# TensorE's loop cut at another place of the tile, with its matmul steps at fixed slots of the instruction blocks

## Chip, cores and metric

One NeuronCore of a Trainium2 chip runs the whole kernel. The metric is the device time of one execution in microseconds; lower is better.

## What is computed

x is 8 sequences of 2048 rows of 512 float32 values. One layer of causal linear attention with 16 heads of 32, a layer norm, a feed-forward part, and a second layer norm. Cut to its core, the reference is:

```python
q = exp(x @ Wq.T + bq); k = exp(x @ Wk.T + bk); v = x @ Wv.T + bv     # per head of 32
kv = cumsum(k[:, :, :, None] * v[:, :, None, :], axis=1)
k1 = cumsum(k, axis=1)
out = einsum('zsD,zsDd->zsd', q, kv) / sum(q * k1)
x = layernorm(x + out @ Wo.T + bo)
h = x @ weight @ aux_weight1 @ aux_weight2
x = layernorm(x + tanh(h + bias))
```

## The kernel before

A tile is 128 rows of one sequence. There are 128 tiles: NI = 16 positions times B = 8 sequences, and the eight sequences take turns, so tile t is position t // 8 of sequence t % 8. The running sums of a sequence (state, k1) stay on chip.

Each of the five engines has its own program, and semaphores alone tie them together. SyncE issues all the DMAs. VectorE does the scan of K, the transposes, the reciprocal, the sums and the norm statistics. ScalarE copies out of PSUM, takes exp and tanh, and applies the norms. GpSimd masks the scores and makes the low halves of split operands. A float32 product of 512 x 512 weights is done as three passes over rounded operands: high times high, high times low and low times high (`three_pass`, lines 309 to 315, lines 312 to 314 of it are the three matmuls). Each of its four steps k has three matmuls of 512 columns, and each matmul is two instructions of the engine, a weight load and the multiplication, so a step is 6 instructions.

`slot(c, k)` of the TensorE program (line 349) works on tile k of chunk c in this order:

- the denominators of the tile before and its product with the state (`denominators`, lines 368 and 372);
- the scores of the tile (line 425);
- the product of the masked scores of the tile before with V (`attend`, line 381);
- the state update of the tile two back (line 436);
- Q and K: one block each of the projections of the tiles four ahead (lines 450 and 459);
- V of the tile (line 467), the output projection of the tile before (line 396), the feed-forward product of the tile two back (line 408).

The first four groups are many small matmuls, 32 weight loads and 32 multiplications to a product; I call them the small part. The last five are `three_pass` calls, 24 instructions each.

Each engine runs its slots through `run_slots`: tiles -8 to 7 are written out, then a loop over chunks 1 to 13 has eight slots as its body (tiles 8 to 111), then tiles 112 to 129 are written out. In the compiled program before, TensorE's body is 3632 instructions: 453 to a tile (440 weight loads and multiplications and 13 waits of their own, the other waits ride on a matmul) and eight for the loop (the hint and five register updates at its head, an addition and the branch at its end). Within a tile the small part takes instructions 0 to 325, Q 326 to 351, K 352 to 376, V 377 to 400, the output projection 401 to 426 and the feed-forward 427 to 452.

The loop on TensorE:

```python
with nc.Fori(1, NI - 2, engines=(engine.engine,), hint_back_edge=True) as it:
    c = Chunk(it, engine)
    for k in range(B):
        slot(c, k)
```

Of the kernel before, what the change touches and what calls it, by code (L numbers as in the profile page):

```python
# [26 lines left out]
def linear_attention_ffn_kernel(nc, x, wqT, wkT, wvT, woT, bq, bk, bv, bo, w, a1T, a2, bf, out):  # L27
# [5 lines left out]
    P = 128  # L33
# [23 lines left out]
    with ctx:  # L57
# [250 lines left out]
        def _(pe):  # L308
            def three_pass(out, statH, statL, movH, movL):

                for k in range(NK):
                    nc.tensor.matmul(out, statH(k), movH(k), start=(k == 0), stop=False)  # L312
                    nc.tensor.matmul(out, statH(k), movL(k), start=False, stop=False)  # L313
                    last = nc.tensor.matmul(out, statL(k), movH(k), start=False, stop=(k == NK - 1))  # L314
                return last
# [33 lines left out]
            def slot(c, k):  # L349
                b = k % QUAD  # L350
                s = (k // QUAD) % 2
                ns = 1 - s
                cols = slice(b * P, (b + 1) * P)
                att = c.exists(k)
                prev = c.exists(k - 1)
                ffn = c.exists(k - 2)
                proj = c.exists(k + 4)
                heads = [(g, j, slice(g * HD, (g + 1) * HD), slice(j * HD, (j + 1) * HD))
                         for g in range(NK) for j in range(HG)]

                def denominators(n):

                    ts, tcols = (n // QUAD) % 2, slice(n % QUAD * P, (n % QUAD + 1) * P)

                    wait_before(pe, (qk1_ready, c.count(n + 1)), (o_ready, c.count(n)),
                                (state_ready, c.state_count(n - 1)))
                    for g, j, quarter, h in heads:
                        last = nc.tensor.matmul(den_ps[quarter, j, :], ones[h, :], qk1[h, g, :], start=True, stop=True)  # L368
                    last.then_inc(den_done, 1)
                    if c.reads_state(n):  # L370
                        for g, j, quarter, h in heads:
                            nc.tensor.matmul(num_ps[quarter, j, :], state[h, n % B, g, :], QT[h, ts, g, tcols],  # L372
                                             start=True, stop=False, skip_group_check=True)

                def attend(n):
                    wait(pe, v_ready, c.count(n + 1))
                    wait(pe, masked, c.count(n + 1))
                    for j in range(HG):
                        for g in range(NK):
                            f0 = g * P + j * HD  # L380
                            last = nc.tensor.matmul(num_ps[g * HD:(g + 1) * HD, j, :], V[:, n % 2, f0:f0 + HD],  # L381
                                                    A[:, n % 2, j, g, :], start=not c.reads_state(n),
                                                    stop=True, skip_group_check=True)
                    last.then_inc(num_done, 1)

                def output_projection():
                    if not ffn:
                        pe.wait_ge(woh_ready, 1)
                        pe.wait_ge(wol_ready, 1)
                    wait(pe, oh_ready, c.count(k))  # L390
                    wait(pe, ol_ready, c.count(k))

                    if att:
                        wait(pe, scores_out[3], c.count(k + 1))
                    wait(pe, r_ready, c.count(k - 1))
                    three_pass(oproj_ps, lambda f: oH[:, f, :], lambda f: oL[:, f, :],
                               lambda f: WoH[:, f, :], lambda f: WoL[:, f, :]).then_inc(oproj_done, 1)

                def feed_forward():
                    wait(pe, x1h_ready, c.count(k - 1))  # L400
                    wait(pe, x1l_ready, c.count(k - 1))

                    if proj:
                        wait(pe, q_ready, c.count(k + 5))
                    elif att:
                        wait(pe, scores_out[0], c.count(k + 1))
                    wait(pe, z_ready, c.count(k - 2))
                    three_pass(ffn_ps, lambda f: x1H[:, f, :], lambda f: x1L[:, f, :],
                               lambda f: WfH[:, f, :], lambda f: WfL[:, f, :]).then_inc(ffn_done, 1)

                if att and prev:
                    denominators(k - 1)
# [14 lines left out]
                if att and prev:  # L428
                    attend(k - 1)
# [10 lines left out]
                if proj:  # L440
# [15 lines left out]
                    if att:  # L456
# [4 lines left out]
                               lambda f: xTL[:, ns, f, :]).then_inc(kproj_done, 1)  # L461
                if att:
# [4 lines left out]
                    three_pass(v_ps, lambda f: xTH[:, s, f, cols], lambda f: xTL[:, s, f, cols],  # L467
                               lambda f: WvH[:, f, :], lambda f: WvL[:, f, :]).then_inc(v_done, 1)
                if att and not c.exists(k + 1):
                    denominators(k)  # L470
                    attend(k)
# [364 lines left out]
```

## Time and profile before

| | |
|---|---|
| median of 3 runs | 2349.64 us (2347.27 to 2354.92) |
| the profiled execution, its own time | 2354.96 us |
| its span in the trace | 2353.2 us |
| mean granted TensorE clock | 0.991 |
| PE busy | 2250.8 us, 96% |
| PE weight loads busy | 1833.2 us, 78% |
| DVE, POOL, ACT busy | 69%, 55%, 43% |

The profiled execution is the longest of those shown, 5.3 us over the median of the runs. A matmul's end in the trace is modelled, so the intervals between the starts of instructions are the safer measure, and the busy share of PE says only that it is seldom without work. Instructions themselves come from device memory by a DMA queue of their own, the page's queue of kind "instruction": its 235 packets of together 3.85 MB are 16 KB each, 256 instructions of 64 bytes. I call 256 instructions that begin at a multiple of 256 a block.

### The profile page before, as it was taken

To read this page: it belongs to the slowest core of one execution; us is meant where nothing else is said; L and a number is where in the kernel's file an instruction comes from. 1 tells how busy PE (TensorE), PEld (TensorE's weight loads), DVE (VectorE), ACT (ScalarE), POOL (GpSimd) and SP (SyncE) were. 2 spreads that over 40 slices of the span, in tenths; PEclk is the share of its full clock that TensorE was granted. 3 is DMA by queue.
4 is the path that set the end of the run, shared out by engine and by line. 5 is a ranking of instruction groups with operands and counts; after the bars stand their busy time and mean duration, and the time that the engine had idled before them with its cause. 6 is when DMAs were issued, how large, how long until landed. Compare 5 with 4: busy or idle time off the path is not lost.

```text
span 2353.2 us, 71216 instructions
## 1 busy us (share of the span) xinstructions
PE 2250.8 (96%) x27784; PEld 1833.2 (78%) x27784; DVE 1620.6 (69%) x2444; ACT 1012.5 (43%) x1683; POOL 1289.1 (55%) x1797
## 2 busy tenths in 40 slices
PE   3999999999999999999999999999999999999985
PEld 2778887878888888887878788787888878788864
DVE  3477776776776767767767767677777677677674
ACT  2344444444444444444444444444444444444442
POOL 1255555556555555555555555555555655555553
PEclk9999999999999999999999999999999999999997
DMA  5133333333333333333333333333333333333221
GB/s 156 46 101 107 108 108 107 104 108 109 105 110 103 109 109 104 109 108 100 113 105 105 105 107 109 104 105 107 110 104 109 109 100 107 111 101 113 69 68 55
DMA packets 294453, 242.74 MB, mean 103 GB/s; under 512 B 33329, under 2 KB 225841, under 8 KB 294193
## 3 DMA queue, kind: packets, MB, share of 16 engines
q1 hardware_dynamic: 294192, 238.69, 32.5%
q8 instruction: 235, 3.85, 0.7%
q14 instruction: 26, 0.20, 0.0%
HBM read 139.99 MB, written 98.57 MB: 101 GB/s over the span
## 4 chain that ended last, share of the span: by engine, by line
PE 94%; issue 2%; DVE 2%; ACT 1%; DMA 1%; POOL 1%; SPq 0%; POOLq 0%; DVEq 0%; ACTq 0%
PE SC L312 26%; PE SC L313 25%; PE SC L314 24%; PE SC L425 6%; PE ND L381 5%; PE ND L372 3%; PE ND L368 2%; PE ND L436 2%; DVE o L670 0%; PE ND L312 0%; PE ND L313 0%; PE ND L314 0%; DMA KT<-wkT 0%; DMA QT<-wqT 0%; ACT A L552 0%
## 5 line engine op out<-in xcount | busy, mean ns | idle before, releaser
L756 POOL TENSOR_SCALAR_AFFINE_SELECT A<-A 128x512 f32<-128x512 f32 x512 | 327.8, 674 | 313.2 <-ACT A L552 313.1
L670 DVE RECIPROCAL o<-ND 128x512 f32<-128x512 f32 x128 | 427.8, 3342 | 1.1 <-PE ND L381 0.9
L727 DVE TENSOR_TENSOR xres<-SC,xres 128x512 f32<-128x512 f32 x128 | 88.6, 692 | 457.0 <-PE SC L314 456.8
L750 POOL TENSOR_TENSOR oL<-o,oH 128x512 fp32r<-128x512 f32 x128 | 166.1, 1298 | 324.8 <-ACT oH L531 324.8
L542 ACT ACTIVATE WK<-xres,shift,rstd 128x512 f32<-128x512 f32 x128 | 104.4, 816 | 530.4 <-POOL shift L796 530.4
L552 ACT ACTIVATE A<-SC 128x512 f32<-128x512 f32 x512 | 264.7, 603 | 48.7 <-PE SC L425 48.6
L312 PE MATMUL SC<-xTH,WqH 128*128 128x512 f32 x512 | 211.3, 413 | 31.4 <-POOL xTL L785 27.3
L785 POOL TENSOR_TENSOR xTL<-xin,xTH 128x512 fp32r<-128x512 f32 x128 | 165.7, 1295 | 100.8 <-ACT xTH L580 100.7
L312 PE MATMUL SC<-WfH,x1H 128*128 128x512 f32 x512 | 201.4, 393 | 14.4 <-issue 7.8
L683 DVE TENSOR_TENSOR_SCAN WK<-ones,k,KT 128x128 f32<-128x128 f32 x512 | 207.7, 468 | 9.9 <-PE ND L368 9.9
L313 PE MATMUL SC<-xTL,WqH 128*128 128x512 f32 x512 | 201.2, 393 | 13.0 <-issue 13.0
L557 ACT ACTIVATE QT<-SC,bcol 128x512 f32<-128x512 f32 x128 | 88.4, 691 | 289.8 <-PE SC L314 289.8
L312 PE MATMUL SC<-WoH,oH 128*128 128x512 f32 x512 | 201.0, 393 | 9.8 <-issue 7.8
L312 PE MATMUL SC<-xTH,WkH 128*128 128x512 f32 x512 | 200.3, 391 | 7.7 <-DVE WkL L616 7.7
L312 PE MATMUL SC<-WvH,xTH 128*128 128x512 f32 x512 | 199.6, 390 | 2.7 <-ACT A L552 2.7
L314 PE MATMUL SC<-xTH,WqL 128*128 128x512 f32 x512 | 201.4, 393 | 0.0
L313 PE MATMUL SC<-WfL,x1H 128*128 128x512 f32 x512 | 200.8, 392 | 0.0
L314 PE MATMUL SC<-WfH,x1L 128*128 128x512 f32 x512 | 200.5, 392 | 0.0
L314 PE MATMUL SC<-WoH,oL 128*128 128x512 f32 x512 | 200.4, 391 | 0.0
L313 PE MATMUL SC<-WoL,oH 128*128 128x512 f32 x512 | 200.2, 391 | 0.0
L313 PE MATMUL SC<-xTL,WkH 128*128 128x512 f32 x512 | 200.0, 391 | 0.0
L314 PE MATMUL SC<-xTH,WkL 128*128 128x512 f32 x512 | 199.9, 390 | 0.0
(100 smaller groups left out, 5025.0 us busy)
## 6 DMA issues: line engine op xcount, KB each, us to landing
xin<-x SPq DMA_DIRECT2D x512, 64.0 KB, 1.8
xres<-x SPq DMA_DIRECT2D x128, 256.0 KB, 2.6
x_rows<-WK SPq DMA_DIRECT2D x128, 256.0 KB, 2.9
WK<-x_rows SPq DMA_DIRECT2D x512, 64.0 KB, 2.0
out<-WK SPq DMA_DIRECT2D x128, 256.0 KB, 2.1
k_rows<-WK SPq DMA_DIRECT2D x120, 256.0 KB, 2.0
WK<-k_rows SPq DMA_DIRECT2D x480, 64.0 KB, 1.9
QT<-wqT SPq DMA_DIRECT2D x4, 256.0 KB, 4.5
```

The source lines that it names most:

```text
L312: nc.tensor.matmul(out, statH(k), movH(k), start=(k == 0), stop=False)
L313: nc.tensor.matmul(out, statH(k), movL(k), start=False, stop=False)
L314: last = nc.tensor.matmul(out, statL(k), movH(k), start=False, stop=(k == NK - 1))
L381: last = nc.tensor.matmul(num_ps[g * HD:(g + 1) * HD, j, :], V[:, n % 2, f0:f0 + HD], A[:, n % 2, j, g, :], start=not c.reads_state(n), st ...
L425: last = nc.tensor.matmul(SC[:, j, g * P:(g + 1) * P], KT[h, s, g, cols], QT[h, s, g, cols], start=True, stop=True)
L542: nc.scalar.activation(x1[:, n % 2, :], xres[:, n % 2, :], ACT.Identity, bias=shift[:, 0:1], scale=rstd[:, 0:1]).then_inc(x1_ready, 1)
L552: nc.scalar.activation(A[:, k % 2, j, :, :].rearrange("p g q -> p (g q)"), SC[:, j, :], ACT.Copy).then_inc(scores_out[j], 1)
L670: nc.vector.reciprocal(o[:, :, :], den_ps).then_inc(recip_ready, 1)
L683: last = nc.vector.tensor_tensor_scan(qk1[:, g, :], ones[:, 0:1].to_broadcast([P, P]), KT[:, s, g, cols], k1[:, k % B, g:g + 1], ALU.mult, ...
L750: nc.gpsimd.tensor_tensor(oL[:, :, :], o[:, :, :], oH[:, :, :].bitcast(F32), ALU.subtract).then_inc(ol_ready, 1)
L756: last = nc.gpsimd.affine_select(out=A[:, k % 2, j, :, :], in_=A[:, k % 2, j, :, :], compare_op=ALU.is_ge, fill=0.0, base=0, pattern=[[0, ...
L785: nc.gpsimd.tensor_tensor(halves[1], xin[:, m % XIN, :].rearrange("p (t g q) -> p g t q", t=HG, q=HD), halves[0].bitcast(F32), ALU.subtrac ...
```

## The change

The TensorE `slot` is cut into three functions: `small` (denominators to state update), `queries_and_keys`, and `values_output_ffn`. The order of the instructions that compute is the same over the whole program. The loop on TensorE begins one tile's small part, Q and K later: these of tile 8 are written out ahead of it, the body is V, output projection and feed-forward of tile k and then small part, Q and K of tile k + 1, and after the loop the first written tile begins at V. The other engines keep `run_slots` as it was.

Inside the loop, and only there (`c.static()` is false), padding is asked for: V begins at slot 0 of a block of 256, the output projection at 40, the feed-forward at 80, and the steps k = 1, 2, 3 of each begin 10, 20 and 30 slots after its start. `addr_align` fills the slots up to the place with no-operations. `head_slot` puts the first instruction of the loop at slot 232 of a block, the loader branching over that gap once.

```diff
-            def three_pass(out, statH, statL, movH, movL):
+            def three_pass(out, statH, statL, movH, movL, place=None):
                 for k in range(NK):
+                    if place is not None and k > 0:
+                        pe.addr_align(256, offset=place + 10 * k, max_nops=255)
                     nc.tensor.matmul(out, statH(k), movH(k), start=(k == 0), stop=False)
...
+            def values_output_ffn(c, k):
...
+                v_place, o_place, f_place = (None, None, None) if c.static() else (0, 40, 80)
+
+                def align(place):
+                    if place is not None:
+                        pe.addr_align(256, offset=place, max_nops=255)
+
+                def output_projection():
+                    align(o_place)
...
+                def feed_forward():
+                    align(f_place)
...
                 if att:
+                    align(v_place)
...
-            run_slots(pe, slot, 8, 2, {-3: multiply_aux, -2: multiply_weight, -1: multiply_bv})
+            setup = {-3: multiply_aux, -2: multiply_weight, -1: multiply_bv}
+            for t in range(-8, B):
+                c, k = Chunk(t // B), t % B
+                small(c, k)
+                queries_and_keys(c, k)
+                values_output_ffn(c, k)
+                if t in setup:
+                    setup[t]()
+
+            small(Chunk(1), 0)
+            queries_and_keys(Chunk(1), 0)
+            with nc.Fori(1, NI - 2, engines=(pe.engine,), hint_back_edge=True, head_slot={pe.engine: 232}) as it:
+                c = Chunk(it, pe)
+                for k in range(B):
+                    values_output_ffn(c, k)
+                    small(c, k + 1)
+                    queries_and_keys(c, k + 1)
+            for t in range(NT - 2 * B, NT + 2):
+                c, k = Chunk(t // B), t % B
+                if t > NT - 2 * B:
+                    small(c, k)
+                    queries_and_keys(c, k)
+                values_output_ffn(c, k)
```

## Rows read from the trace of the kernel before

**Rows 1.** Page, part 4: the chain that ended last, shares of the span

```profile
PE 94%; issue 2%; DVE 2%; ACT 1%; DMA 1%; POOL 1%; SPq 0%; POOLq 0%; DVEq 0%; ACTq 0%
```

**Rows 2.** Groups of instructions: busy us, mean ns | idle before us <-releasers

```profile
L313 PE MATMUL SC<-xTL,WqH 128*128 128x512 f32 x512 | 201.2, 393 | 13.0 <-issue 13.0
...
L313 PEld LDWEIGHTS SC<-WoL,oH 128*128 128x128 f32 x512 | 96.9, 189 | 20.0
```

**Rows 3.** Timeline, PE, 1059 to 1066: start, us, instructions, [idle before <-releaser]

```profile
1059.83 0.52 PE L372 MATMUL ND<-QT,state 32*32 32x128 f32 x4
1060.77 0.50 PE L372 MATMUL ND<-QT,state 32*32 32x128 f32 x28 [0.43 <-issue]
1061.22 1.17 PE L425 MATMUL SC<-QT,KT 32*128 32x128 f32 x32
...
1063.65 0.47 PE L312 MATMUL SC<-xTH,WqH 128*128 128x512 f32 x1
1065.36 0.39 PE L313 MATMUL SC<-xTL,WqH 128*128 128x512 f32 x1 [1.23 <-issue]
```

**Rows 4.** Timeline, PE, a tile without idle time

```profile
1079.18 0.75 PE L372 MATMUL ND<-QT,state 32*32 32x128 f32 x32
1079.87 1.17 PE L425 MATMUL SC<-QT,KT 32*128 32x128 f32 x32
...
1082.31 0.47 PE L312 MATMUL SC<-xTH,WqH 128*128 128x512 f32 x1
1082.61 0.39 PE L313 MATMUL SC<-xTL,WqH 128*128 128x512 f32 x1
...
1087.85 0.39 PE L312 MATMUL SC<-WvH,xTH 128*128 128x512 f32 x1
...
1090.12 0.39 PE L313 MATMUL SC<-WvL,xTH 128*128 128x512 f32 x1
1090.34 0.39 PE L314 MATMUL SC<-WvH,xTL 128*128 128x512 f32 x1
1090.57 0.39 PE L312 MATMUL SC<-WoH,oH 128*128 128x512 f32 x1
```

**Rows 5.** Timeline, PE: first scores in the loop, two later tiles, first scores after it

```profile
223.40 1.17 PE L425 MATMUL SC<-QT,KT 32*128 32x128 f32 x32
...
1114.33 1.17 PE L425 MATMUL SC<-QT,KT 32*128 32x128 f32 x32
...
1201.33 1.17 PE L425 MATMUL SC<-QT,KT 32*128 32x128 f32 x32
...
2044.28 1.17 PE L425 MATMUL SC<-QT,KT 32*128 32x128 f32 x32 [1.10 <-issue]
```

**Rows 6.** Timeline, PE, 990.5 to 994.5: the stall in the fifth tile of the body

```profile
992.86 0.37 PE L436 MATMUL ND<-V,WK 128*32 128x32 f32 x24
993.65 0.27 PE L436 MATMUL ND<-V,WK 128*32 128x32 f32 x8 [0.42 <-issue]
```

**Rows 7.** Queues: packets, MB, share of 16 engines; windows 0:2353.2 (page) and 1061.22:1201.33

```profile
q8 instruction: 235, 3.85, 0.7%
...
q8 instruction: 15, 0.25, 0.8%
```

**Rows 8.** Queues, windows of 0.1 us from 990.9, 1057.3, 1062.9, 1066.8, 1080.9, 1084.9

```profile
q8 instruction: 1, 0.02, 81.7%
...
q8 instruction: 1, 0.02, 122.4%
...
q8 instruction: 1, 0.02, 60.0%
...
q8 instruction: 1, 0.02, 77.2%
...
q8 instruction: 1, 0.02, 92.8%
...
q8 instruction: 1, 0.02, 76.8%
```

**Rows 9.** Queues, windows of 0.1 us from 1185.0 and 1198.3

```profile
q8 instruction: 1, 0.02, 89.9%
...
q8 instruction: 1, 0.02, 64.6%
```

**Rows 10.** Timeline, PE, 1200 to 1206

```profile
1200.88 0.50 PE L372 MATMUL ND<-QT,state 32*32 32x128 f32 x28 [0.30 <-issue]
...
1205.46 0.40 PE L313 MATMUL SC<-xTL,WqH 128*128 128x512 f32 x1 [1.23 <-issue]
```

More of the change, by code:

```diff
@@ L347, in multiply_bv, with denominators @@
                 pe.wait_ge(consts_ready, 1)
-            def slot(c, k):
-                b = k % QUAD
+            heads = [(g, j, slice(g * HD, (g + 1) * HD), slice(j * HD, (j + 1) * HD))
+                     for g in range(NK) for j in range(HG)]
+            def denominators(c, n):
+                ts, tcols = (n // QUAD) % 2, slice(n % QUAD * P, (n % QUAD + 1) * P)
+                wait_before(pe, (qk1_ready, c.count(n + 1)), (o_ready, c.count(n)),
+                            (state_ready, c.state_count(n - 1)))
+                for g, j, quarter, h in heads:
+                    last = nc.tensor.matmul(den_ps[quarter, j, :], ones[h, :], qk1[h, g, :], start=True, stop=True)
+                last.then_inc(den_done, 1)
+                if c.reads_state(n):
+                    for g, j, quarter, h in heads:
+                        nc.tensor.matmul(num_ps[quarter, j, :], state[h, n % B, g, :], QT[h, ts, g, tcols],
+                                         start=True, stop=False, skip_group_check=True)
@@ new lines, in attend @@
+            def attend(c, n):
+                wait(pe, v_ready, c.count(n + 1))
+                wait(pe, masked, c.count(n + 1))
+                for j in range(HG):
+                    for g in range(NK):
+                        f0 = g * P + j * HD
+                        last = nc.tensor.matmul(num_ps[g * HD:(g + 1) * HD, j, :], V[:, n % 2, f0:f0 + HD],
+                                                A[:, n % 2, j, g, :], start=not c.reads_state(n),
+                                                stop=True, skip_group_check=True)
+                last.then_inc(num_done, 1)
@@ L351, in slot, with small @@
+            def small(c, k):
                 s = (k // QUAD) % 2
-                ns = 1 - s
-                cols = slice(b * P, (b + 1) * P)
+                cols = slice(k % QUAD * P, (k % QUAD + 1) * P)
                 att = c.exists(k)
                 prev = c.exists(k - 1)
[L356 to L409, printed above, removed]
@@ L412, in slot @@
                 if att and prev:
-                    denominators(k - 1)
+                    denominators(c, k - 1)
                 if att:
```

39 lines of the change are left out of this document (34 added, 5 removed).

## Prediction

> **What bounds the kernel now.** I read the chain that ended last first: 94% of it is PE, 2% is "issue", time in which the engine waited for nothing that the profile shows [rows 1]. So the matmul stream sets the time and every gap in it counts in full. The groups view puts one such gap on one line: the second matmul of Q, 13.0 us in all, released by "issue" [rows 2]. The timeline shows where: once in eight tiles, L313 comes 1.71 us after L312 [rows 3], where a calm tile has 0.30 [rows 4]: 1.41 us lost. The same tile lost 0.70 before, 1.39 us from the first L372 to the scores [rows 3] against 0.69 [rows 4].
>
> The places are those of block boundaries. Within the body the gap in L372 is after 32 + 4 pairs, two waits and the six instructions of the head: instruction 80. The gap in Q is after 6 + 328 + 2 = 336, 256 later. Counting on by 256, number 2128 is instruction 310 of the fifth tile, after 24 of the 32 pairs of L436, and there the third gap is [rows 6]. All other boundaries meet no gap. So a gap is the wait for the next block of instructions, and the head of the loop now lies at slot 176.
>
> **What one block costs.** A packet of the instruction queue is one block. In a window of 0.1 us its share times 1.6 us is how long it took: 1.31, 1.96, 0.96, 1.24, 1.48 and 1.23 us for the six of rows 8. PE goes on about 1.5 us after the packet's end: 1062.9 + 0.96 to 1065.36 is 1.50, 1057.3 + 1.96 to 1060.77 is 1.51, 990.9 + 1.31 to 993.65 is 1.44 [rows 3, 6, 8]. Where the sequencer has to wait for each block, packets start 4.0 us apart: 1062.9 and 1066.8, 1080.9 and 1084.9 [rows 8]. So the next block is asked for when the sequencer enters the present one, and takes about 4 us. A block of small matmuls lasts some 3 us on PE, one with three-pass work up to 10. At the back edge two short blocks follow each other (80 instructions, then 256 small ones), and this is why both gaps are there. The packet at 1185.0 is followed by none until 1198.3 [rows 9], and PE runs past instruction 80 at 1200.88 [rows 10]; the next packet comes later. So the one of 1185.0 brought the loop's first block, 13 us ahead: the hint works, and the one of 1198.3 brought the second.
>
> The Trainium skill (Runtime: NRT & Kernel Launch, "Instruction fetch mechanics") says that fetch in a straight line hides behind the sequencer's issue pace, and that a taken branch to a block outside the window stalls for a fetch. The gap in the fifth tile [rows 6], far from any branch, disagrees with the first half.
>
> **The sum of what is there.** From the scores of tile 8 to those of tile 112 are 2044.28 - 223.40 = 1820.88 us [rows 5]. A calm tile takes (1114.33 - 1079.87) / 2 = 17.23 us [rows 4, 5], and 104 of them 1791.9. So 29.0 us are gaps: 140.11 us for eight tiles [rows 3, 5] against 137.8, some 2.2 us an iteration. That is all the change can win in the loop.
>
> **Part by part.** *Length of the code.* From V at slot 0: 24 instructions and 16 no-operations to 40; output projection 26 and 14 to 80; feed-forward 26 and 10 ends at 116; small part 326 to 442, Q to 468, K to 493; 19 no-operations to 512. So a tile is exactly two blocks with 59 no-operations, in 12 groups. One boundary is at V, the other 7 instructions into the scores. An iteration fetches 17 blocks, not 15 [rows 7].
>
> *Gaps inside the body.* The block that begins at V holds V, output projection, feed-forward and the denominators: the three of them 36 matmuls of 0.227 us (1090.12 to 1090.57 is two of them [rows 4]), 8.2 us, and the next block is there after about 4. The one that begins in the scores has 2.4 us of small work and then Q and K: V starts 7.98 us after the scores [rows 4]. Both are twice what a block needs. The gap of the fifth tile goes: nothing is late in its place.
>
> *The back edge.* Two fetches now lie in a row here too: the loop's first block (slots 232 to 255) is asked for on entering the last block, in the scores, and the block of V on entering the first. Let S be the start of the scores. In the calm tile before, a boundary lies exactly at the scores, and the packet follows at S + 1.03 [rows 4, 8]. The next packet 4.0 later; its length 1.2, and 1.5 to the matmul: S + 7.7. V is due at S + 7.98. So 0.3 us to spare on the mean, and with the longest packet, 1.96, a gap of 0.5. The sequencer must be able to stand at the end of K while PE is early in Q, nearly 50 instructions ahead. It can: the packet of 1084.9 was asked for on entering the block at instruction 389, in V, when PE was in the first steps of Q, 38 or more instructions behind. I take 0.2 us for each of the 12 back edges, 2.4 us; the ends are 0 and 1.0.
>
> The Trainium skill (Advanced Engine Details and Errata, "Engine Queue Depths") gives TensorE a queue of 64; that agrees with the 38 or more.
>
> *No-operations.* No row shows one. The nearest are two waits that are already met, between V and the output projection: the step there is 0.23 us (1090.34 to 1090.57), the same as inside V (1090.12 to 1090.34) [rows 4]. So an instruction of the sequencer alone costs nothing while matmuls stand in the queue. The other end: each group keeps the next weight load from overlapping, 0.189 us [rows 2], 12 groups, 104 tiles: 236 us. A gain is excluded, PE runs these steps at their pace already. I take 0, which is the nearer row.
>
> *Entry and exit.* The branch over the padding is taken once, with the queue full of Q and K: 0. At the exit the tile before lost about 1.7 us, the largest part in one gap of 1.10 [rows 5]; the fetch had been told the loop's head. Now the exit has K behind it and the 5.5 us of Q and K on PE as cover. I leave 0.5. Tiles before 8 and after 112 keep their code; their boundaries fall elsewhere, 0 give or take 1.5 us. No DMA, no wait and no instruction of another engine moves. Their slack is enough: the tiles between 1079.87 and 1114.33 already run at 17.23 with nothing to catch up in [rows 4, 5].
>
> **Sum.** 29.0 - 2.4 - 0.5 = 26.1 us less. On the profiled execution 2354.96 gives 2328.9. That execution was 5.3 us over the median; the median of 2349.64 gives 2323.6, and I say 2324.
>
> **Rivals.** *A, as forecast*, 0.62: 2318 to 2328.
>
> *B, the chain at the back edge is longer*, 0.15. After the gap at 1060.77 the next packet began 2.1 us later, not 1.5 as after 1065.36 [rows 3, 8]; with branch, register updates and 18 no-operations in the head, the same could be usual here. Then 0.6 to 1.2 us stay at each edge, 12 times 0.9 is 10.8, and the time is 2332.
>
> *C, the change doesn't do what it says, or the gaps are only moved*, 0.08: a wait of another engine takes their place, as the gaps now give everyone 2 us an iteration to catch up. Against it: the calm tiles. 2343 to 2356.
>
> *D, no-operations hold up the matmul stream*, 0.10. Each group would have to cost only 26.1 / (12 x 104) = 0.02 us for the gain to be gone; at 0.05 the kernel takes 62 us more, less 26: 2386. For it: nothing; against it: the waits between V and output projection.
>
> *E, the head isn't fetched ahead at this place*, 0.05. A branch to a block not there costs a whole fetch, and then V's block another: a block is 1.5 + 1.2 + 1.5 = 4.2 us from request to matmul, and with the branch reached early in Q, at S + 3, V starts at S + 11.4, a gap of 3.4 us. Twelve of them are 41 us against 29.0 - 0.5 won: 2362. Against it is the packet of 1185.0. The Trainium skill's rule on branches (Runtime: NRT & Kernel Launch, "Instruction fetch mechanics") is this case.
>
> **Chances and range.** Faster by over 0.3% (7 us, about what a measurement of this kernel can tell from no change) are A and B, 0.77; same is C, 0.08; slower D and E, 0.15. The range runs from 2316 (no gap left, and 1.5 us more of the ends) to 2345, which takes in A, B and the edge of C.
>
> **What the profile after would show.** The second matmul of Q has no "issue" before it. The fifth tile has no gap in L436. Two instruction packets a tile, one about 1 us after the scores began and one 4 us later, and 26 more in all. The step from one matmul of V to the next is 0.227 across a group of no-operations; 0.4 there would be D. A gap before the first matmul of V in every eighth tile, up to 0.5 us, is A; near 1, B; over 3, E. A loop of 104 tiles longer than 1800 us would make the sum wrong.

## The result and the profile after

The changed kernel takes 2328.61 us (median, 2327.62 to 2329.22), the kernel before, in the runs now set beside it, 2352.28 us. The ratio is 0.9901, with a 95% interval of 0.9879 to 0.9922: 1.0% faster. The forecast was 2324 us with a range of 2316 to 2345. Its profiled execution took 2327.62 us, 27.3 less than that of before. I call the return from the end of the loop's body to its head the edge (there are 12, for 13 rounds), and a tile without a gap calm.

| | before | after |
|---|---|---|
| profiled execution, its time and its span | 2354.96, 2353.2 us | 2327.62, 2325.9 us |
| scores of tile 8 to scores of tile 112 | 1820.88 us | 1796.67 us |
| scores of tile 112 to the end of the span | 308.9 us | 307.0 us |
| start of the span to scores of tile 8 | 223.4 us | 222.2 us |
| PE busy | 2250.8 us | 2242.6 us |

24.2 of the 27.3 us come from the 104 tiles of the loop. PE's busy time is 8 us less; with modelled ends it counts a part of the gaps. A small part of the rest is work: the product of tile 7 with the state, 32 pairs of L372 with a state of zeros, is in the loop before and is left out now that this small part is written out (27752 matmuls, 27784 before). The description of the change ahead, that the order of the computing instructions is the same over the whole program, holds but for these.

The page of after, lines of its parts 1, 3, 4 and 5. Where before had 235 blocks and 2% "issue" [rows 1, 7], there are 260 and 1%:

```profile
PE 2242.6 (96%) x27752; PEld 1830.6 (79%) x27752; DVE 1603.7 (69%) x2444; ACT 1008.9 (43%) x1683; POOL 1290.4 (55%) x1797
...
q8 instruction: 260, 4.26, 0.8%
...
PE 94%; DVE 2%; issue 1%; ACT 1%; DMA 1%; POOL 1%; SPq 0%; POOLq 0%; DVEq 0%; ACTq 0%
...
L315 PE MATMUL SC<-xTL,WqH 128*128 128x512 f32 x512 | 201.0, 393 | 0.0
```

The last line is the second matmul of Q, with no idle time before it; before it had 13.0 us [rows 2]. The lines of the code moved: L312 to L314 of before are L314 to L316 now, L368 is L361, L425 is L400, L436 is L411.

The timeline of PE in after, one edge and the tile behind it (start, duration, instructions):

```profile
1050.56 1.17 PE L400 MATMUL SC<-QT,KT 32*128 32x128 f32 x32
...
1053.00 0.47 PE L314 MATMUL SC<-xTH,WqH 128*128 128x512 f32 x1
1053.31 0.39 PE L315 MATMUL SC<-xTL,WqH 128*128 128x512 f32 x1
...
1058.32 0.39 PE L316 MATMUL SC<-xTH,WkL 128*128 128x512 f32 x1
1058.83 0.50 PE L314 MATMUL SC<-WvH,xTH 128*128 128x512 f32 x1
...
1068.22 1.17 PE L400 MATMUL SC<-QT,KT 32*128 32x128 f32 x32
...
1075.96 0.39 PE L316 MATMUL SC<-xTH,WkL 128*128 128x512 f32 x1
1076.19 0.39 PE L314 MATMUL SC<-WvH,xTH 128*128 128x512 f32 x1
...
1076.64 0.39 PE L316 MATMUL SC<-WvH,xTL 128*128 128x512 f32 x1
1076.87 0.39 PE L314 MATMUL SC<-WvH,xTH 128*128 128x512 f32 x1
```

At the edge K to V takes 0.51 us, in the next tile 0.23: 0.28 lost, and the tile of the edge is 17.66 us long, 0.43 over a calm one. From 1076.64 to 1076.87 lie four no-operations, and the step is the 0.23 of every other one. Over all 12 edges the tiles are 2.4 us longer than calm ones (0 to 0.46 each). All other tiles of the loop take 17.22 to 17.28 us, but for the last.

The last is where TensorE's loop was thought to end. The timelines of after at tile 112, of PE and of VectorE:

```profile
2018.91 1.17 PE L400 MATMUL SC<-QT,KT 32*128 32x128 f32 x32 [1.79 <-issue]
```

```profile
2014.96 0.18 DVE L780 BATCH_NORM_AGGREGATE mv<-bnst 128x2 f32<-128x6 f32 x1
2018.02 0.69 DVE L726 TENSOR_TENSOR WK<-SC,bfbc 128x512 f32<-128x512 f32 x1 [2.88 <-issue]
```

In after, these scores are the last pass of TensorE's loop body, not the first code behind it, and still they come 1.8 us late, as in before [rows 5]. They wait for z_ready, which VectorE's L726 sets, and VectorE comes out of its own loop just there, idle for 2.88 us. I return to this with e7.

### The profile page after: what moved, and what is told of

The parts are those of the page before. It is cut to its first block, busy times and chain, and to the rows that moved or that the text cites. A ratio compares the mean times of both kernels' runs of the same rounds, so it can differ in the third digit from the quotient of the medians.

```text
span 2325.9 us, 77275 instructions
## 1 busy us (share of the span) xinstructions
PE 2242.6 (96%) x27752; PEld 1830.6 (79%) x27752; DVE 1603.7 (69%) x2444; ACT 1008.9 (43%) x1683; POOL 1290.4 (55%) x1797
## 4 chain that ended last, share of the span: by engine, by line
PE 94%; DVE 2%; issue 1%; ACT 1%; DMA 1%; POOL 1%; SPq 0%; POOLq 0%; DVEq 0%; ACTq 0%
PE SC L314 26%; PE SC L315 25%; PE SC L316 25%; PE SC L400 6%; PE ND L374 5%; PE ND L365 3%; PE ND L361 2%; PE ND L411 2%; DVE o L719 0%; PE ND L314 0%; PE ND L316 0%; PE ND L315 0%; DMA KT<-wkT 0%; DMA QT<-wqT 0%; ACT A L601 0%
## 5 line engine op out<-in xcount | busy, mean ns | idle before, releaser
L314 PE MATMUL SC<-xTH,WqH 128*128 128x512 f32 x512 | 210.4, 411 | 30.5 <-POOL xTL L834 27.0
L314 PE MATMUL SC<-WfH,x1H 128*128 128x512 f32 x512 | 200.7, 392 | 14.4 <-issue 7.9
L314 PE MATMUL SC<-WoH,oH 128*128 128x512 f32 x512 | 201.0, 393 | 9.7 <-issue 7.8
L314 PE MATMUL SC<-xTH,WkH 128*128 128x512 f32 x512 | 200.0, 391 | 6.7 <-DVE WkL L665 6.7
L314 PE MATMUL SC<-WvH,xTH 128*128 128x512 f32 x512 | 200.7, 392 | 3.1 <-ACT A L601 2.7
L316 PE MATMUL SC<-xTH,WqL 128*128 128x512 f32 x512 | 200.7, 392 | 0.0
L316 PE MATMUL SC<-WoH,oL 128*128 128x512 f32 x512 | 200.4, 392 | 0.0
L316 PE MATMUL SC<-WfH,x1L 128*128 128x512 f32 x512 | 200.2, 391 | 0.0
L316 PE MATMUL SC<-xTH,WkL 128*128 128x512 f32 x512 | 199.6, 390 | 0.0
```

## The experiments

For each kernel the table has its median, its ratio to before with the interval, and the time from the scores of tile 8 to those of tile 112 in its profile, where 1791.9 is a loop without gaps. This last number is steadier than the time of a run and tells more. Each ratio is to the runs of before made beside that kernel, whose medians were 2352.28 for after and 2348.81 to 2350.76 for e1 to e12, so times of different rows are compared by their ratios.

| kernel | us | ratio | loop, us |
|---|---|---|---|
| before | 2352.28 | | 1820.9 |
| after | 2328.61 | 0.9901 (0.9879 to 0.9922) | 1796.7 |
| e1 rotation only | 2354.29 | 1.0023 (1.0013 to 1.0034) | 1818.4 |
| e2 places only | 2330.99 | 0.9924 (0.9903 to 0.9945) | 1797.8 |
| e3 one group of 59 | 2372.65 | 1.0104 (1.0087 to 1.0121) | 1838.2 |
| e4 no hint | 2382.67 | 1.0146 (1.0115 to 1.0176) | 1847.9 |
| e5 head at 0, V at 8 | 2327.88 | 0.9912 (0.9891 to 0.9932) | 1794.3 |
| e6 before, head at 0 | 2350.01 | 1.0009 (0.9998 to 1.0021) | 1818.7 |
| e7 e5 and VectorE's head | 2325.59 | 0.9902 (0.9886 to 0.9919) | 1793.1 |
| e8 three blocks a tile | 3993.57 | 1.7006 (1.6972 to 1.7040) | 3461.7 |
| e9 e6 with light loads | 2350.09 | 0.9995 (0.9986 to 1.0005) | 1820.4 |
| e10 before, head at 40 | 2338.42 | 0.9950 (0.9933 to 0.9966) | 1805.5 |
| e11 groups of 16 and 43 | 2328.01 | 0.9901 (0.9885 to 0.9918) | 1795.1 |
| e12 all exits | 2325.79 | 0.9895 (0.9879 to 0.9912) | 1793.3 |

The expectations name two theories. The first is that of the prediction: a gap is the wait for a block of instructions (FETCH). Its rival is that it matters only what work stands around the branch (EDGE).

### e1 and e2: which half of the change does it

e1 takes all padding out and keeps the rotation; e2 keeps the places, moves the slot of the head to 110, and puts the loop back to where it was.

```diff
-                v_place, o_place, f_place = (None, None, None) if c.static() else (0, 40, 80)
+                v_place, o_place, f_place = (None, None, None)
-            with nc.Fori(1, NI - 2, ..., head_slot={pe.engine: 232}) as it:
+            with nc.Fori(1, NI - 2, ...) as it:
```

> The changed kernel without any padding: neither places in the tile nor a slot for the head. By the count of its compiled program the head lies at slot 233 and block boundaries lie 17, 273 instructions after V of the first tile of the body, and so on every 256; the last before the back edge is in K of the eighth tile. FETCH (gaps are the wait for a block, about 4 us from request to use): at the edge three blocks follow each other in Q and K, and V's second block comes about 1.8 us late, 12 times 1.8 is 22; the third tile of the body has a boundary 59 instructions into its small part and one 256 later, as the fifth tile had before, about 0.45 us times 13 is 6. So about 28 us over the changed kernel's 2328.6 less its 2.4 of edge gaps: 2350 to 2358, no better than before. EDGE (it matters only whether the branch comes in front of small matmuls or behind K): as the changed kernel, 2327 to 2331.

Measured: 2354.29, a little slower than before. The edge costs 1.1 to 1.7 us each time, in two gaps, one before V and one within it, and the pair of boundaries in the third pass of the body up to 0.8, 0.35 on the mean. The rotation alone wins nothing. The timeline of PE in e1; V begins at 1069.00, and the block boundary 17 instructions into V is where the second gap lies:

```profile
1068.18 0.39 PE L316 MATMUL SC<-xTH,WkL 128*128 128x512 f32 x1
1069.00 0.49 PE L314 MATMUL SC<-WvH,xTH 128*128 128x512 f32 x1 [0.43 <-issue]
...
1071.63 0.40 PE L316 MATMUL SC<-WvH,xTL 128*128 128x512 f32 x1 [0.53 <-issue]
```

```diff
-                    values_output_ffn(c, k)
-                    small(c, k + 1)
-                    queries_and_keys(c, k + 1)
+                    small(c, k)
+                    queries_and_keys(c, k)
+                    values_output_ffn(c, k)
```

(and the head at slot 110, and the first small part, Q and K no longer written out; the first diff is e1, this one e2.)

> The loop body of the kernel before (small part first, feed-forward last) with the places of the changed kernel; the head lies at slot 110, so that the small part begins at 116 and V of each tile at 0 of a block. FETCH: every tile has its boundaries at V and in the scores, no gaps inside the body; at the edge the block after the head's is needed 146 instructions after the head instead of 80, some 0.3 us of PE later, and the block after it is needed only at V. The 1.41 us in Q goes, of the 0.70 in L372 about 0.4 stay, now before the scores: 13 times 0.4 is 5, against the 2.4 of the changed kernel: 2330 to 2334. EDGE: the branch is where it was in the kernel before, so its loss stays, 2350 to 2356.

Measured: 2330.99, and the loop 1797.8 us. So the places, with a slot for the head, bring 23 of the 24 us of the loop, with the branch ahead of the small matmuls as in the kernel before. No run has the places without a slot for the head. What is left at the edge is now in the scores, where the boundary lies (1.66 us for the group that takes 1.17):

```profile
1190.48 1.66 PE L400 MATMUL SC<-QT,KT 32*128 32x128 f32 x32
```

EDGE is wrong in both runs, FETCH right in both within its ranges.

### e5 and e4: how many fetches lie in the way of V

e5 moves the head to slot 0 and V to slot 8 (output projection 48, feed-forward 88), so that V lies in the head's own block. e4 takes the hint away.

```diff
-                v_place, o_place, f_place = (None, None, None) if c.static() else (0, 40, 80)
+                v_place, o_place, f_place = (None, None, None) if c.static() else (8, 48, 88)
-            with nc.Fori(..., head_slot={pe.engine: 232}) as it:
+            with nc.Fori(..., head_slot={pe.engine: 0}) as it:
```

> The changed kernel with the head of the loop at slot 0 of a block and V, output projection and feed-forward at 8, 48 and 88, so that V lies in the head's own block and is not behind a second fetch; only one block has to come between scores and V. FETCH: the gap before V at the back edge (0.2 us on the mean, up to 0.45) is gone, the 104 tiles of the loop take 1794.3 instead of 1796.7 us, the time is 2324 to 2328. EDGE (branch, register updates and no-operations cost it themselves): the gap stays, 1796.7 and 2327 to 2330.

Measured: the loop took 2017.77 - 223.50 = 1794.27 us, and all 12 edge tiles are calm (17.22 to 17.26). It has 248 blocks against 260, one fewer at each edge than after. The two lines, of the timeline of PE in e5:

```profile
223.50 1.17 PE L400 MATMUL SC<-QT,KT 32*128 32x128 f32 x32 [0.51 <-issue]
...
2017.77 1.17 PE L400 MATMUL SC<-QT,KT 32*128 32x128 f32 x32 [1.61 <-issue]
```

So what was left at the edge of the changed kernel is the second fetch, not the branch. In the time of the runs 2.4 us can't be told from after's; in the loop they can.

```diff
-            with nc.Fori(1, NI - 2, engines=(pe.engine,), hint_back_edge=True, head_slot={pe.engine: 232}) as it:
+            with nc.Fori(1, NI - 2, engines=(pe.engine,), head_slot={pe.engine: 232}) as it:
```

> The changed kernel without the hint on the back edge. FETCH: the head's block is asked for only at the branch, which the sequencer reaches some 4.8 us after the scores began, and V's block only after that, 2 times 4.2 us; V is due 8.0 us after the scores, so it comes about 5 us late, 12 times 5 is 62: 2375 to 2395. If the branch is reached earlier, at 3 us, 41 us: 2370. EDGE without regard to the fetch: at most the branch's own cost, 2328 to 2335.

Measured: 2382.67; the edge tiles are 2.8 to 5.4 us longer, 4.4 on the mean. This is rival E's mechanism made real, and it costs more than the change wins. But the 4.4 us are two things. V itself comes 2.6 to 3.8 us late, 3.2 on the mean, where 5 were expected. In eight of the twelve edges the matmuls after the wait then run at the lower clock of 1.2 GHz for some us (granted clock 0.50, 0.43 us from one to the next instead of 0.23), as below. Without this second part, 1.2 us an edge, the time would be some 2368 us (an estimate), under the range of 2375 to 2395; that it fell inside is luck. V after one edge in e4, and the windows view over some of it (columns: us, busy of the engines, granted clock, DMA):

```profile
1083.52 0.50 PE L314 MATMUL SC<-WvH,xTH 128*128 128x512 f32 x1 [2.64 <-issue]
...
1085.30 0.63 PE L316 MATMUL SC<-WvH,xTL 128*128 128x512 f32 x1
1085.73 0.63 PE L314 MATMUL SC<-WvH,xTH 128*128 128x512 f32 x1
```

```profile
1084.50:1087.00 2.50, 2.50 (x7) 1.93 (x6) 0.00 (x0) 0.00 (x0) 0.83 (x1) 0.50 0.63 160
```

### e3, e8 and e11: what a no-operation costs

> The changed kernel with a place for V alone: the 59 no-operations of a tile stand in one group between K and V, none among the matmuls. GROUPS HOLD UP MATMULS (the price of no-operations lies in their groups): fewer groups, faster by what they cost. SEQUENCER TIME: in the changed kernel the packets asked for at the scores and at V start 5.0 to 5.25 us apart in a tile, with 19 no-operations between, and 4.0 apart where none stand; so a no-operation takes the sequencer about 0.05 us. With 59 there, the distance becomes about 7 us, V is reached 6.8 us after the scores began where it is due at 8.0, and the time stays 2327 to 2331. If the distance stays at 5, a no-operation costs nothing that can be seen.

```diff
-                v_place, o_place, f_place = (None, None, None) if c.static() else (0, 40, 80)
+                v_place, o_place, f_place = (None if c.static() else 0), None, None
-                               lambda f: WvH[:, f, :], lambda f: WvL[:, f, :], v_place).then_inc(v_done, 1)
+                               lambda f: WvH[:, f, :], lambda f: WvL[:, f, :]).then_inc(v_done, 1)
```

Measured: 2372.65, 44 us slower than the changed kernel with the same number of no-operations, and a miss for both expectations. Every tile but the loop's first and those at the edge takes 17.7 us, 0.47 more, all of it before V. Timeline of PE in e3:

```profile
1114.03 0.39 PE L316 MATMUL SC<-xTH,WkL 128*128 128x512 f32 x1
1114.61 0.47 PE L314 MATMUL SC<-WvH,xTH 128*128 128x512 f32 x1 [0.19 <-issue]
```

At the edges, where a group of 18 stands in the head instead of the 59, the tiles take 17.22 to 17.60. The packets did not move apart as I expected either: around these tiles they start at 1084.75, 1089.75, 1102.25 and 1107.5, still in pairs 5 us apart, but the first of a pair comes only after V. The one at 1102.25 (queues view of e3, a window of 0.25 us), to which I return with e9:

```profile
q8 instruction: 1, 0.02, 23.9%
```

> As e5_head_at_0, with output projection and feed-forward at 176 and 216 instead of 48 and 88: a tile is three blocks, with 315 no-operations instead of 59, 132 of them between V and output projection and 147 between K and V. It is rival D taken to where it must show. At 0.05 us for one (see e3) the sequencer is done with K about 4.8 us after the scores began and with the group 7.4 us later, at 12.2, where V is due at 8.0: 3 to 5 us a tile, 104 tiles: 2650 to 2850. At one in 0.017 us, the pace of a sequencer that hands on one instruction every 20 cycles (an estimate from the Trainium skill, Runtime: NRT and Kernel Launch, Instruction fetch mechanics, with its clock from Advanced Engine Details and Errata, Clock Domains), the group takes 2.5 us and V is in time: 2327 to 2335. If no-operations cost nothing at all: 2327 to 2330.

```diff
-                v_place, o_place, f_place = (None, None, None) if c.static() else (8, 48, 88)
+                v_place, o_place, f_place = (None, None, None) if c.static() else (8, 176, 216)
```

Measured: 3993.57 us, worse than the worst I had put down. The expectation counted the group before V alone, but each of its tiles pays for all groups. It gives the price. Timeline of PE in e8:

```profile
1095.26 0.76 PE L314 MATMUL SC<-WvH,xTH 128*128 128x512 f32 x1 [6.79 <-issue]
...
1106.25 0.77 PE L314 MATMUL SC<-WoH,oH 128*128 128x512 f32 x1 [5.81 <-issue]
```

Both starts follow an empty queue, and between them the sequencer hands on 24 instructions of V, two waits and 12 + 132 no-operations: 10.99 us. If all count the same, 0.065 us each; if only the no-operations count, 0.076. I use 0.07. The 256 more in a tile cost 16.0 us, 0.063 each, so the no-operations can account for all of it. The clock fell as well: over these 11 us the granted clock was 0.66, a mean over stretches at 1.2 and at 2.4 GHz, with PE idle for more than half of them, and 1.00, 2.4 GHz, a little later. What the clock alone costs here no run separates (the windows view of e8, columns: us, busy of the engines, granted clock, DMA):

```profile
1095.26:1106.25 10.99, 5.17 (x12) 3.79 (x13) 0.00 (x0) 1.81 (x3) 1.26 (x1) 0.66 0.07 25
1113.70:1117.20 3.50, 3.50 (x161) 3.01 (x161) 3.28 (x8) 2.54 (x5) 0.89 (x3) 1.00 0.22 80
```

The Trainium skill (Runtime: NRT & Kernel Launch, "Instruction fetch mechanics") names about 20 cycles for the sequencer to hand on an instruction, 0.017 us with its clock of 1.2 GHz (Advanced Engine Details and Errata, "Clock Domains"). A no-operation of padding takes four times that here; the page calls its number a floor, so the trace does not contradict it, but it is not the price of this kind.

> As e3_one_group but with a place for the output projection too: the 59 no-operations stand in two groups, 16 before the output projection and 43 before V. In e3 V came 0.47 us late in every tile, and in e8 144 no-operations with 26 instructions took 11.0 us, so about 0.073 us for one. 16 fewer before V are 1.2 us, which turns 0.47 late into 0.7 early: no gap, 2327 to 2331, loop of 104 tiles 1796 to 1798. If it is the length of one group in the queue and not the sequencer's time that matters, V is still late, by some 0.2 to 0.4 us a tile: 2348 to 2370.

```diff
-                v_place, o_place, f_place = (None if c.static() else 0), None, None
+                v_place, o_place, f_place = (None, None, None) if c.static() else (0, 40, None)
```

Measured: 2328.01, the loop 1795.1 us (2019.36 - 224.31), as fast as the changed kernel. Sixteen no-operations taken from the group before V and put before the output projection save 44 us. So what counts is not the number of no-operations, nor how many groups there are, but whether the sequencer reaches the next matmul before PE has emptied the queue: 59 times 0.07 is 4.1 us, which was 0.47 too much in e3, so the last of K is issued about 3.7 us before V is due; 43 take 3.0 and are covered. This 3.7 is an estimate (3.4 to 4.0 with 0.065 and 0.076), not read from a row.

### e6, e9 and e10: where the head should lie

> The kernel before with one thing changed: the head of TensorE's loop lies at slot 0 of a block and not at 176. No padding in the body, loop cut where it was. FETCH: the next block is needed 256 instructions after the head and not 80, when feed-forward and 250 small instructions have covered it, no gap; the block after comes in the next tile. Left are the pairs of boundaries wholly inside a small part: instructions 53 and 309 of the second tile, as before 0.5 us, and 33 and 289 of the sixth, about 0.3. 13 times 0.8 and the exit are 12 us of gaps in the loop instead of 29: 2331 to 2337. EDGE: the branch is where it was, 2346 to 2354.

```diff
-            with nc.Fori(1, NI - 2, engines=(engine.engine,), hint_back_edge=True) as it:
+            with nc.Fori(1, NI - 2, engines=(engine.engine,), hint_back_edge=True,
+                         head_slot={engine.engine: head} if head is not None else None) as it:
```

(head = 0 for TensorE, none for the others.)

Measured: 2350.01, a clear miss. The two gaps of before at the edge are gone and the pair in the second tile costs the 0.5 us expected, the one in the sixth nothing, but a new gap of 0.8 to 2.0 us stands before the very first matmul of the body: the head's own block is late. Timeline of PE in e6:

```profile
1061.17 0.39 PE L315 MATMUL SC<-WfH,x1L 128*128 128x512 f32 x1
1062.68 0.51 PE L369 MATMUL ND<-WK,ones 32*32 32x128 f32 x32 [1.11 <-issue]
```

The block before the head's is entered 407 instructions into the eighth tile, in the output projection. By "asked for on entering" the packet of the head had to start near 1056. It started at 1059.0 (queues view of e6, a window of 0.25 us):

```profile
q8 instruction: 1, 0.02, 32.1%
```

That is one microsecond after x1L of GpSimd was done (1056.64 + 1.31 = 1057.95), for which the sequencer waits before feed-forward. Timeline of POOL in e6, then in e9:

```profile
1056.64 1.31 POOL L779 TENSOR_TENSOR x1L<-WK,x1H 128x512 fp32r<-128x512 f32 x1
```

```profile
1055.02 1.30 POOL L781 TENSOR_TENSOR x1L<-WK,x1H 128x512 fp32r<-128x512 f32 x1
```

> As e6_before_head_0, but inside the loop the loads of xin and of xres bring a quarter of their bytes (the first 128 columns of each row block); the rest of these tiles keeps old values, so the output of tiles in the loop is not the reference's. In e6 the first block of the loop came late: its packet started 13.7 us after the last scores, 3 us after TensorE had begun the output projection in which the block before is entered, and PE stood 1.2 us before the first denominators in each of 13 edges. The packets of all kernels start 0 to 1.5, 4 to 7 or 13.5 to 15 us after the scores, none in the 8 to 13 us in which the loads of xin and xres run. QUEUED BEHIND LOADS: the packet waits for the data of these loads; with a quarter of it the packet starts about 10.5 to 11.5 us after the scores and the gap goes, 13 times 1.2 is 15: 2333 to 2338. ASKED FOR LATE (the hinted block is asked for only when the sequencer is past the wait before feed-forward, 1.0 us before the packet): the gap stays, 2346 to 2352.

```diff
-                        sp.dma_start(xin[...].rearrange("p (t f) -> p t f", t=HG), x_b[n % B, c.it + n // B, j])
+                        part = slice(0, HG if c.static() else 1)
+                        sp.dma_start(xin[...].rearrange("p (t f) -> p t f", t=HG)[:, part], x_b[n % B, c.it + n // B, j][:, part])
-                    sp.dma_start(xres[:, k % 2, :], x_t[k % B, c.it + k // B])
+                    part = slice(0, D if c.static() else P)
+                    sp.dma_start(xres[:, k % 2, part], x_t[k % B, c.it + k // B][:, part])
```

In the loop the kernel leaves out three quarters of these loads, so its output there is not the reference's. Measured: 2350.09, the loop 1820.4, the gap still there (1.69 us at the edge that has 1.11 in e6). The queue for data moved this much in 40 us of e9, and then of e6:

```profile
q1 hardware_dynamic: 3984, 3.15, 24.2%
```

```profile
q1 hardware_dynamic: 4983, 4.23, 33.2%
```

The packet of the head came at 1057.25, 0.93 us after x1L (1055.02 + 1.30 = 1056.32); queues view of e9, a window of 0.25 us:

```profile
q8 instruction: 1, 0.02, 46.7%
```

These loads are not what the packet waits for: with less of them the packet starts no earlier in the tile. (The expectation's remark that no packet of any kernel starts 8 to 13 us after the scores is wrong: after each edge of the changed kernel one starts 9.7 to 10.4 us after them.) Over all 12 edges the packet starts 0.96 to 2.3 us after x1L is done in e6 and 0.95 to 1.8 in e9, ten of the twelve within 1.3 us in both. The same is seen in e3: x1L was done at 1099.93 + 1.30 = 1101.23, and the packet came at 1102.25. So the request does not always leave at once when a block is entered. One explanation fits: where the sequencer runs into an unmet wait some 20 to 50 instructions behind the boundary, the request leaves about 1 us after that wait is met. It is not shown. x1L is done about 12.7 us after the scores in every kernel, so no run moved it against the rest of the tile, and anything else at that place would do as well. And in 13 of the 91 tiles of e3 that are neither the loop's first nor at an edge the packet comes before x1L is done, 9.2 to 11.3 us after the scores. Whether the sequencer itself does the asking, and can't while it waits, is left open too.

> The kernel before with the head of TensorE's loop at slot 40. The last boundary before the back edge lies 367 instructions into the eighth tile, in K; the packet asked for there starts 4 to 6 us after the scores and brings the head in time. The block after the head is needed 210 small instructions in. So neither of the two edge gaps, and no gap before the first denominators as in e6. Inside the body there are boundary pairs 52 and 308 in one small part (0.5 us, as before) and 72 and 328 in another (0.3). 13 times 0.8 and the 1.7 of VectorE's exit are 12 us of gaps against 29: 2330 to 2336. If the place of the blocks is not what matters at the edge: 2346 to 2354, like e6.

```diff
-            run_slots(pe, slot, 8, 2, {..., -1: multiply_bv}, head=0)
+            run_slots(pe, slot, 8, 2, {..., -1: multiply_bv}, head=40)
```

Measured: 2338.42, the loop 2027.53 - 222.05 = 1805.5 us. One number in the kernel before, without padding in its body, takes away 15 of the 29 us of gaps in the loop, and all edges are calm. The two pairs of boundaries inside small parts are left: 0.2 to 0.5 us in the third tile, 0.1 to 0.8 in the seventh, 0.8 an iteration and 10.4 us in all, as the sum had them. With the 1.6 of the exit and 1.5 spread in hundredths over the other tiles 13.6 us of gaps are left, not 12. The range of 2330 to 2336 was 2.4 us too low; before itself took 2350.76 us beside it, 1.1 more than the median that stands ahead.

### e7 and e12: the exits of the other engines

> As e5_head_at_0, and VectorE's loop head at slot 35 of a block, so that its closing branch lies at slot 258, 2 past a boundary, and the code after the loop is in a block that is there. The gap of 1.7 us before the scores of tile 112 is in every kernel so far, whichever way TensorE's loop ends, and VectorE's first instruction after its own exit starts 2.7 to 2.9 us late, with a packet for another engine's instructions in that time. VECTORE'S FETCH: the gap goes, the span of the 104 tiles becomes 1792.6 instead of 1794.3, the time 2325 to 2328, 1.7 less than e5. TENSORE'S EXIT: nothing changes, 1794.3. A mispredicted branch costs VectorE its time even with the code present: nothing changes either.

```diff
             run_slots(dve, slot, 8, 3, {-7: split_wq, -5: split_wk, -4: split_aux,
-                                       -3: split_a12, -2: split_wv_wf_wo, -1: add_bo})
+                                       -3: split_a12, -2: split_wv_wf_wo, -1: add_bo}, head=35)
```

Measured: 2325.59; the tile before the scores of tile 112 is 17.24 us long, where it was 18.9 in e5 and 19.1 in after. Timelines of e7, PE and then VectorE at its exit:

```profile
2016.27 1.17 PE L401 MATMUL SC<-QT,KT 32*128 32x128 f32 x32
```

```profile
2014.29 0.18 DVE L781 BATCH_NORM_AGGREGATE mv<-bnst 128x2 f32<-128x6 f32 x1 [0.22 <-DVE bnst L779]
2015.37 0.69 DVE L727 TENSOR_TENSOR WK<-SC,bfbc 128x512 f32<-128x512 f32 x1 [0.89 <-PE SC L317]
```

VectorE's first instruction behind its loop is released by PE now, not by "issue", and its idle time is 0.89 us, not 2.88. In after a packet of the other instruction queue (8 KB) starts in that idle time, at 2016.10; in e7 that queue has none from 2010 to 2020. Queues view of after, a window of 0.25 us from 2016:

```profile
q14 instruction: 1, 0.01, 13.7%
```

The loop took 1793.1 us against the 1792.6 expected. So the 1.6 to 1.9 us that every other kernel up to here had were a fetch of VectorE, and the branch that goes the unhinted way costs nothing that shows when the code behind it is there.

> As e7_dve_exit, with the heads of ScalarE's, GpSimd's and SyncE's loops placed so that their closing branches lie 2 past a multiple of 128 slots (slots 83, 51 and 232), and with TensorE's places kept in tiles 112 to 119. What is left of gaps between tiles 112 and 121 in e7 is 1.1 us in tile 114, released by ScalarE, and 0.7 in tile 115, where a block boundary falls into L411. FETCH: both are waits for code after the loop and go in part: 2323 to 2325.5. If ScalarE is late for another reason, only the 0.7 goes: 2324.5 to 2326.

Its edit gives the slots 83, 51 and 232 in the same way and takes the places for TensorE also where `c.it` is NI - 2. Measured: 2325.79, no better than e7. The 1.1 us in tile 114 and the 0.7 in tile 115 went (four things changed at once, so which engine's exit had the 1.1 is not separated), but V behind TensorE's exit now waits 0.93 us, since the places put a boundary in its way there too.

e7 is the fastest kernel by its median, 3.0 us under the changed one, and 3.5 us faster in the loop (1793.1 against 1796.7). But its ratio to its own before is that of the changed kernel (0.9902 and 0.9901), so as a time of the kernel this is not shown; as gaps in the trace it is.

## Why the prediction was right, and where it was not

**The number.** 26.1 us less were forecast and the profiled execution shows 27.3 (2327.6 us against 2328.9). The medians are 23.7 apart, and 2328.61 lies 0.6 above the 2318 to 2328 of rival A, whose mechanism came true. So that the time comes so near the forecast is in part luck: one more run of before moved its median by 2.6 us.

**The bound.** 29.0 us of gaps in the loop were taken as all that there is to win. 24.2 were won and 4.8 are left. e5 and e7 bring the loop to within 2.4 and 1.2 us of the 1791.9. This step holds.

**The gaps are waits for blocks.** It holds: e1, e2, e4, e5 and e10 move the blocks or their fetches with the same matmuls around them, and the gaps follow as counted, to within 0.6 us an edge, but for e4, whose wait is 3.2 us and not 5. e6 is the exception, and it points to a second condition: when the request leaves.

**The gaps inside the body.** None is left in after, as forecast. The prediction's 10 us for the longest block was short: in before, packets 1066.8 and 1080.9 are 14 us apart. Nothing hung on it. In calm tiles of after the two packets start 4.7 to 6.6 us apart, not 4, and there are 25 blocks more, not 26.

**The back edge.** The sum had 0.2 us an edge, 2.4 in all; the 12 edge tiles of after are 2.4 us longer. The chain behind the number was right in kind and too short in one link. Over the 12 edges the first packet starts 0.9 to 1.4 us after the scores (1.03 was forecast), the second 3.8 to 5.0 us later, 4.4 on the mean (4.0), and is 0.9 to 1.5 long, 1.1 on the mean (1.2); V goes on 1.3 to 1.8 us after its end (1.5). That is 8.0 us after the scores where the sum had 7.7 and V is due at 7.98, so most edges wait a little, instead of only those with a long packet. The 4.0 was read from two pairs; all 68 close pairs in the loop of before are 3.4 to 4.9 us apart, 4.2 on the mean. The 0.2 us was a choice between 0 and 1.0 and not the outcome of the sum; that it is exact is luck. The edge with the widest pair (queues view of after, windows of 0.25 us from 1051.25 and 1056.25, where a share times 4 us is the length; the packets start at 1051.46 and 1056.50):

```profile
q8 instruction: 1, 0.02, 27.3%
...
q8 instruction: 1, 0.02, 23.4%
```

**No-operations.** I took 0, from two waits that were already met, and it holds for the groups as the change has them. As a general step it was wrong: they take the sequencer about 0.07 us each, and only the queue ahead of PE hides it. Rival D had the wrong mechanism (a group that keeps a weight load from overlapping) but the right worry: with all 59 in one place the kernel would have been slower than before (e3). Its point of decision is not 0.02 us a group; it is about 3.7 us of no-operations in the stretch between K and V. The cover that I should have named is the queue of matmuls that PE still has when the sequencer is done with K.

**Entry and exit.** I put 1.7 us at the exit down to TensorE's own fetch and kept 0.5. It was VectorE's exit, untouched by the change, and 1.85 us stayed (19.08 us for that tile). This is the term of the sum that was mis-sized: 29.0 - 2.4 - 1.8 is 24.8, and 24.2 were measured in the loop; the rest is spread in hundredths over the other tiles. The row was marked "issue" on PE, and I did not ask whose semaphore the scores wait for.

**The rest of the time.** The profiled executions differ by 27.3 us, the medians by 23.7. Outside the loop 1.2 us went before it and 1.9 behind it.

**The rivals.** B's mechanism is there in part (packets up to 5.0 apart), its price is not (0.46 us at most). C: no other engine took the place of the gaps. E is e4.

**The order of the steps.** The prediction took rotation and places as one. The places with a slot for the head do nearly all (e2), such a slot alone does 15 of the 24 us (e10), and what the rotation adds (1.1 us of the loop) is within what e5's choice of two numbers adds again.

## What to carry to other kernels

When a long loop's engine shows short "issue" gaps at the same instructions in every iteration, count instructions from one gap to the next: if the distances are multiples of 256, the engine waits for its code, and the cure is to put boundaries where slow instructions follow. Try the cheap form first: the slot of the loop's head alone won half of it here at 40 (e10), and nothing at 0 (e6), so count where the boundaries fall and look at the trace. Padding was paid in the sequencer's time here, 0.07 us a piece, so spread it among slow instructions and keep any one group well below what the queue ahead of the engine covers. A gap at a loop's end may belong to another engine's loop.

## What the runs showed of the hardware that I had not expected

- A no-operation of padding costs 0.065 to 0.076 us of TensorE's sequencer (e8), and 59 in a row before V cost 0.47 us a tile where 43 cost nothing (e3, e11).
- The packet of the next block does not always follow the entry of a block at once: in e6 and e9 it starts about 1 us after x1L is done, also with a quarter of the input loads, and so it does in 78 of 91 tiles of e3. Why is not shown.
- Without the hint V comes 3.2 us late at an edge on the mean, and the tile is 4.4 longer, since after the wait matmuls ran at 1.2 GHz in eight of twelve edges (e4); with the hint and V in the head's block an edge costs nothing (e5).
- VectorE was idle 2.7 to 2.9 us when it left its loop, and 0.9 with its branch just past a boundary; on TensorE's path that is 1.6 to 1.9 us (e7).
